# Cross-attention of a two-layer Perceiver on one core: decay scans in another place, high halves of the context tiles by ACT, and a re-ordered start

## The reference, cut to what matters

```python
x = x + L0_xattn(layernorm(x), ctx_2048, Wq, Wk, Wv)      # x (2,128,256), ctx (2,2048,256)
# 32 heads of 8: q, k = per-head rmsnorm(x Wq.T), rmsnorm(ctx Wk.T); v = ctx Wv.T
# out = softmax(q k.T * 8**-0.5) v
x = x + L0_attn(layernorm(x), ...)
x = x + L0_ffn(layernorm(x), ...)
x = x + L1_xattn(layernorm(x), ctx_2048, decay, W_in, b_in, W_out, b_out, gamma, beta)
#   K = sigmoid(decay); s_t = K * s_{t-1} + (W_in ctx_t + b_in); mean over t of W_out s_t + b_out
x = x + L1_attn(layernorm(x), ...)
x = x + L1_ffn(layernorm(x), ...)
```

## Time and profile before

| what | us |
|---|---|
| median of three runs | 450.17 |
| the profiled execution's own time | 449.79 |
| its span, first to last instruction | 448.0 |
| PE busy | 399.9 (89%) |
| DVE busy | 310.7 (69%) |
| ACT busy | 250.4 (56%) |
| POOL busy | 221.3 (49%) |

### The profile page before, as it was taken

The page is one execution under the profiler, slowest core; times in us unless marked ns, Lnnn a source line. Parts: engine busy times, 40 slices in busy tenths (PEclk is TensorE's granted clock), DMA queues, the critical chain, the costliest instruction groups (busy, mean ns, idle before and its releaser), DMA issues.

```text
span 448.0 us, 12553 instructions
## 1 busy us (share of the span) xinstructions
PE 399.9 (89%) x5149; PEld 333.5 (74%) x5149; DVE 310.7 (69%) x697; ACT 250.4 (56%) x494; POOL 221.3 (49%) x269
## 2 busy tenths in 40 slices
PE   6769999999999999879979977789789888999997
PEld 4546666677667777678979955668679877889996
DVE  5677878887888786557798876574998967322221
ACT  2447878778887888775545514521923044544541
POOL 2267656666666773334544620510489742544440
PEclk9979999999999999999999989999899999999999
DMA  4076651543311101620000080250000052000000
GB/s 149 0 262 229 206 172 45 164 127 91 105 32 44 30 15 47 247 113 1 0 1 2 1 321 3 79 244 1 0 2 1 1 227 102 1 0 2 0 2 23
DMA packets 10537, 34.67 MB, mean 77 GB/s; under 512 B 2160, under 2 KB 7280, under 8 KB 8688
## 3 DMA queue, kind: packets, MB, share of 16 engines
q1 hardware_dynamic: 10336, 33.34, 21.4%
q10 hardware_dynamic: 144, 0.52, 0.5%
HBM read 33.60 MB, written 0.26 MB: 76 GB/s over the span
## 4 chain that ended last, share of the span: by engine, by line
PE 52%; DVE 27%; POOL 10%; ACT 5%; issue 4%; DMA 1%; SPq 0%; DVEq 0%; POOLq 0%; ACTq 0%
PE ps L1075 7%; PE ps L1576 7%; PE ps L1532 6%; PE ps L1061 6%; PE ps L1546 3%; PE ps L395 3%; DVE sb_big L1315 2%; PE ps L1563 2%; POOL sb_arena L984 2%; PE ps L456 2%; PE ps L381 2%; DVE sb_arena L1325 2%; PE ps L746 2%; POOL sb_mid L998 2%; DVE sb_big L1313 2%
## 5 line engine op out<-in xcount | busy, mean ns | idle before, releaser
L1499 ACT ACTIVATE sb_arena<-ps 128x1024 f32<-128x1024 f32 x128 | 123.4, 1020 | 26.4 <-PE ps L1563 26.3
L1576 PE MATMUL ps<-sb_arena 128*25 128x128 f32 (+1 forms) x2048 | 69.4, 276 | 0.3 <-ACT sb_arena L1499 0.3
L1576 PEld LDWEIGHTS ps<-sb_arena 128*25 128x25 f32 (+1 forms) x2048 | 50.7, 98 | 7.7 <-ACT sb_arena L1499 0.8
L1532 PE MATMUL ps<-sb_halves 128*128 128x512 f32 x192 | 55.4, 425 | 0.9 <-DVE sb_arena L1325 0.9
L1105 POOL TENSOR_TENSOR sb_halves<-sb_big,sb_halves 128x704 fp32r<-128x704 f32 x20 | 33.7, 1687 | 38.8 <-ACT sb_halves L1099 38.8
L485 POOL TENSOR_TENSOR sb_halves<-sb_big,sb_halves 128x256 fp32r<-128x256 f32 x32 | 23.7, 760 | 44.9 <-ACT sb_halves L469 44.9
L1171 DVE SCALAR_TENSOR_TENSOR sb_arena<-ps,sb_w_q,sb_arena 128x176 f32<-128x176 f32 x40 | 15.9, 401 | 42.7 <-ACT sb_arena L1123 42.5
L1532 PEld LDWEIGHTS ps<-sb_halves 128*128 128x128 f32 x192 | 35.3, 197 | 13.5 <-issue 5.9
L1398 POOL TENSOR_TENSOR sb_big<-sb_arena 128x256 f32<-128x256 f32 x31 | 19.0, 613 | 52.3 <-DVE sb_arena L1286 52.3
L1075 PE MATMUL ps<-sb_halves 128*128 128x352 f32 x240 | 42.9, 332 | 2.0 <-POOL sb_halves L1105 2.0
L1075 PEld LDWEIGHTS ps<-sb_halves 128*128 128x128 f32 x240 | 39.1, 189 | 3.3 <-DVE sb_arena L1171 1.7
(11 more groups left out here) (223 smaller groups left out, 871.0 us busy)
## 6 DMA issues: line engine op xcount, KB each, us to landing
sb_big<-in_w_gu SPq DMA_DIRECT2D x2, 3520.0 KB, 11.8
sb_arena<-in_ctx SPq DMA_DIRECT2D x32, 128.0 KB, 2.3
sb_mid<-in_w_down SPq DMA_DIRECT2D x1, 3584.0 KB, 12.7
sb_mid<-in_w_ffn SPq DMA_DIRECT2D x3, 768.0 KB, 5.3
sb_big<-in_w_q SPq DMA_DIRECT2D x2, 1024.0 KB, 6.5
sb_big<-in_w_k SPq DMA_DIRECT2D x2, 1024.0 KB, 7.1
sb_big<-in_w_v SPq DMA_DIRECT2D x2, 1024.0 KB, 6.0
sb_mid<-in_w_o SPq DMA_DIRECT2D x2, 1024.0 KB, 6.0
```

The lines of the kernel that those rows point to most:

```text
L1499: nc.scalar.activation(probs[:, n % P_SLOTS].rearrange("p a g n -> p a (g n)"), ps[:, bank:bank + 2], ACT.Exp, scale=XD ** -0.5).then_inc( ...
L1532: i = T.matmul(ps[:, 7], ctx_half[:, t % 2, c, kt], wkv_half[:, d, kt], start=(n + kt == 0), stop=(n == 2 and kt == KT - 1))
L1576: i = T.matmul(ps[32 * gg:32 * gg + m, 6, j * P:(j + 1) * P], v_sb[:, t % V_SLOTS, 4 * gg + j, head], probs[:, n % P_SLOTS, a, gg], start= ...
```

## The change

Seven edits, all in the cross-attention stage:

1. DVE: the decay rate and the first scan move from behind the packing of tile 1 to the start; the scan of tile t + 2 moves from the head of step t to behind `take_v(t + 2)`, ahead of `mean_squares(t + 2)`.
2. The high half of context tiles 4 to 31 is made by ACT (`split_high`), behind the third exponential of step t for tile t + 4, and no longer by POOL. POOL still makes the low half and waits for the high one.
3. The values of tile 0 are taken by ACT instead of DVE.
4. The queries of the second batch are taken by ACT a little later, behind `key_rstd(0)`.
5. ACT loads its function table ahead of the DMA of `w_xkv`, and issues the DMA of `w_xq` behind it, which SP issued before.
6. PE makes `project(1)` ahead of the transposes of the queries.
7. PE gets 20 more unread matmuls at the start, in groups of 6, 4, 6 and 4.

```diff
-            sp.dma_start(w_xq, io["w_xq"]).then_inc(sem("wq_loaded"), 16)
...
+            decay_rate()
             mean_squares_q(0)
+            decay_weights(0)
             take_k(0)
             norm_q(0)
             mean_squares(0)
             pack_q(0)
-            take_v(0)
             pack_keys(0)
             take_k(1)
             take_keys(0)
             take_v(1)
             mean_squares(1)
+            decay_weights(1)
             pack_keys(1)
-            decay_rate()
-            decay_weights(0)
-            decay_weights(1)
             for t in range(NB):
-                if t + 2 < MB:
-                    decay_weights(t + 2)
                 if t + 2 < NB:
                     take_k(t + 2)
                     take_v(t + 2)
+                    if t + 2 < MB:
+                        decay_weights(t + 2)
                     mean_squares(t + 2)
...
-                if t >= 2:
-                    pool.wait_ge(sem("kv_projected"), t - 1)
-                G.tensor_copy(ctx_half[:, t % 2, 0], ctxT[:, t % CTX_SLOTS]).then_inc(sem("ctx_high"), 1)
+                if t < 4:
+                    if t >= 2:
+                        pool.wait_ge(sem("kv_projected"), t - 1)
+                    G.tensor_copy(ctx_half[:, t % 2, 0], ctxT[:, t % CTX_SLOTS]).then_inc(sem("ctx_high"), 1)
                 pool.wait_ge(sem("ctx_high"), t + 1)
...
+            nc.scalar.preload_act_table_set("natural_log_exp_and_others")
             act.dma_start(w_xkv, io["w_xkv"]).then_inc(sem("wkv_loaded"), 16)
-            nc.scalar.preload_act_table_set("natural_log_exp_and_others")
+            act.dma_start(w_xq, io["w_xq"]).then_inc(sem("wq_loaded"), 16)
...
-            take_queries(1)
+            act.wait_ge(sem("v_cleared"), 1)
+            for r in range(2):
+                i = nc.scalar.copy(v_sb[:, 0, :, 25 * r:25 * r + 8],
+                                   ps[:, 7, 256 + 128 * r:384 + 128 * r].rearrange("p (h d) -> p h d", d=XD))
+            i.then_inc(sem("kv_taken"), 1)
...
+            def split_high(t):
+
+                act.wait_ge(sem(f"ctx_loaded{t % CTX_SLOTS}"), 16 * (t // CTX_SLOTS + 1))
+                act.wait_ge(sem("kv_projected"), t - 1)
+                nc.scalar.copy(ctx_half[:, t % 2, 0], ctxT[:, t % CTX_SLOTS]).then_inc(sem("ctx_high"), 1)
...
             key_rstd(0)
+            take_queries(1)
...
                     exps(SUBS * t + c)
+                    if c == 2 and t + 4 < NB:
+                        split_high(t + 4)
...
             ln_transpose(pe, LN_OF["xattn"], 0)
+            keep_warm(6, 6)
...
+            keep_warm(4, 6)
             open_acc()
+            project(1)
+            keep_warm(6, 0)
             pe.wait_ge(sem("id16_loaded"), 16)
             pe.wait_ge(sem("q_packed"), 1)
             turn_queries(0, 4)
-            project(1)
+            keep_warm(4, 0)
             turn_keys(0)
```

More of the change, by code:

```diff
@@ L1234, in _ @@
             V.memset(xnT[:, :, :, 0:3], 0.0)
-            step(dve, V.memset(v_sb, 0.0))
+            V.memset(v_sb, 0.0).then_inc(sem("v_cleared"), 1)
+            dve.wait_ge(sem("v_cleared"), 1)
             V.memset(v_sb[:, :, :, 8:9], 1.0)
```

## The result

| | kernel before | changed kernel |
|---|---|---|
| median, us | 450.3 (449.66 to 450.70, 4 runs) | 460.46 (458.94 to 461.12, 4 runs) |
| profiled execution, its span | 449.79, 448.0 | 460.0, 458.1 |
| mean granted clock of PE | 0.985 | 0.974 |

At the very start its row is not to be relied on: in the kernel before it says 1.00 from 9 to 12 us, where PE's products take the durations that they have at half clock (experiment 7). So 0.985 is an upper bound.

The account below looks back on a forecast made before the run. No engine alone bounds the cross-attention. With e(t) the start of tile t's third exponential, e(27) = 25.3 + 141.1 + 2.95 - 0.82 = 168.5 against 166.8, less 0.5: +1.2 on 449.79, forecast 451.3 us, range 445.0 to 454.7.

Parts of the forecast that it names:

- the clock: Rival: POOL's stall in packing the second queries reaches PE and brings half clock, 452.8 to 454.3 us; chance 0.16.
- the end: From third exponential of tile 27 to first of tile 29: 6.93 us instead of 7.40, giving back 0.47.
- the steps without a scan: Cross-attention main loop: 14 steps of 5.11 us each, the bare loop of 5.05 plus 0.06.
- the stall: POOL's packing of the second batch's queries stands in the loop once and costs 2.95 us.
- the start: Up to the third exponential of tile 0: it comes at 25.3 us instead of 27.38.
- The loop through POOL, DVE and ACT: Cross-attention main loop: POOL's wait for ACT's cast closes a round of 5.05 us, longer than PE's 4.81.
- the step with a scan: Cross-attention main loop: 13 steps of 5.35 us each, with 0.24 for the scan.
- the two collisions: In the loop's step: packing's last copy on POOL's low half 0.06 us, scan ahead of POOL's next square 0.24.
- a bare loop: Rival: main loop at its bare 5.05 us a step without collisions, 446.7 us; chance 0.21.
- a PE-bound one: Rival: the loop doesn't bind and PE sets 4.81 us a step everywhere, near 438.5 us; chance 0.06.
- the poor start: Rival: unread matmuls delay the first projection and x lands no earlier, 453 us; chance 0.08.
- the whole scans: Rival: each scan in the main loop costs POOL its whole 0.48 us, 3.1 more, 454.4 us; chance 0.05.

Follow-up runs that it names:

- experiment 7: The changed kernel without its 20 added unread matmuls; 460.53 us, ratio 1.021 to the kernel before.
- experiment 3: The changed kernel with ACT's cast behind the first exponential instead of the third; 444.18 us, ratio 0.988 to the kernel before.
- experiment 4: The changed kernel with ACT's cast behind the fourth exponential instead of the third; 480.54 us, ratio 1.068 to the kernel before.
- experiment 8: The changed kernel with matmuls of zeros added into the open accumulator in three idle gaps of PE; 459.22 us, ratio 1.020 to the kernel before.
- experiment 5: The changed kernel with POOL's square of tile 5 ahead of packing the second batch's queries; 458.0 us, ratio 1.016 to the kernel before.
- experiment 2: The kernel before with edit 2 alone, high halves of tiles 4 to 31 by ACT behind the third exponential; 463.0 us, ratio 1.027.
- experiment 1: The changed kernel with all high halves made by POOL again (edit 2 undone); 444.94 us, ratio 0.989 to the kernel before.
- experiment 9: The changed kernel with the cast behind the first exponential, plus zeros in PE's gaps, tile 5's square earlier and DVE's four weight sums moved; 444.8 us, ratio 0.986.
- experiment 10: The changed kernel with high halves on POOL, plus zeros in PE's gaps, tile 5's square earlier and DVE's four weight sums moved; 444.26 us, ratio 0.986.
- experiment 6: The kernel before with the first edit alone, decay rate and scans in their new places; 446.48 us, ratio 0.991.

## Why the prediction was right and wrong

The forecast was 9 us short. In its own terms: the clock, put at nothing in the sum, +3.4 in the steps and +1.35 at the end; the steps without a scan +2.8; the odd step at tile 6 +1.6; the rest of the end +1.6; the stall -0.2; the start -1.7.

**Right: the mechanism.** The loop through POOL, DVE and ACT closes as described and binds both batches (experiments 3 and 4). The forecast 5.05 for its bare length from single rows of before; the second batch shows 0.65 + 0.45 + 0.40 + 0.90 + 0.54 + 0.85 + 0.80 + 0.69 = 5.28. Two terms were small by 0.24 together: low half to product 0.85 for 0.69, because DVE's last copy of the packing falls on it (priced 0.06, cost 0.16), and the cast to POOL 0.54 for 0.46. Over the 14 steps without a scan that and one longer step at tile 16 (5.69) make 2.8 of the missed 7.6.

**Right by two errors: the step with a scan.** 5.35 was forecast and 5.35 came. But the scan cost POOL nothing: the product beside it takes 0.73, the sum 0.73. The scan itself was stretched, from 0.48 to 0.59, and DVE's sum of squares comes 0.71 behind the square instead of 0.65, which no run explains. The 0.24 and 0.06 booked for the two collisions were really the copy's 0.16, the 0.08 between cast and POOL, and this 0.06.

The Trainium skill, SBUF — State Buffer (Who interferes with whom), says that an operation of DVE with two SBUF inputs contends with one of GpSimd that reads SBUF, that the lock is exclusive, and that the order of issue decides who blocks. The forecast left out the order and put the whole 0.48 on POOL. Here POOL's product had started at 81.82 and the scan came at 82.24; by the rule the scan should have waited until 82.55, an estimate of 0.31 from these rows. The trace agrees on who pays and not on the amount: the scan lost 0.11, and POOL kept its 0.73. The cost of a collision has to be given to one of the two, and I gave it to the wrong one.

**Wrong, and the largest: the half clock was priced as a rival and stood at nothing in the sum.** This is the step of the forecast that failed first: 13 x 5.35 takes every step of the first batch at full clock. The forecast named the rival ("Three microseconds at half clock or more cost 1.5 to 3") and gave it 0.16. It came twice in the first batch. Experiment 8, with the gaps filled, shows both: 0.83, 0.92, 0.82 and 0.78 in four steps, 3.35 in all. The text argued that PE's idle 3.44 had come before half clock in the kernel before, and that the stall of 2.95 would go through to PE; both held. The first of the two is not even new: the kernel before has its half clock in the same steps (6.31 and 6.25), hidden in its average of 5.16. So 1.75 of the 3.35 was in the kernel before as well, and only the 1.6 behind the stall is new. The statement "no half clock before 34 us" was wrong too: PE's idle times of 1.49 and 1.02 just ahead of 23.9, with one group of transposes (0.61) between them, came before it here.

**Wrong: a step left out.** At tile 6 the queries of the second batch are transposed in the same bank as the keys; that step took 6.57 before, and 6.98 now, 1.6 above its neighbours. The average of before hid it in 5.16; a sum built from single steps has to list the odd ones.

**Nearly right: the stall.** 2.95 forecast, the step of 8.10 is 2.75 above 5.35. So the first 13 steps are 3.35 (clock) + 1.63 (tile 6) - 0.2 (stall) = 4.8 over the forecast.

**Wrong: the start, by 1.7 to the good, and in part by the luck of the profile.** The forecast priced the unread matmuls as a delay of 0.35 and took PE's first projections at the durations of before. In this profile they ran at full clock (1.13 for 2.08), and e(0) came at 23.62; in the profiles of experiments 4 and 5, with the same start and those durations, it came at 25.31 and 25.16, where the forecast had 25.3. The table load did not hold back the DMA behind it: the DMA was issued at 0.76 while the load ran from 0.73 for 1.28, and DVE's first work on x came 0.13 earlier, not 0.5.

**Wrong: the end.** -0.5 was forecast, +2.5 came. In three parts. The last cast, behind e(27), still holds one more round, so the next two steps take 5.28 + 4.53 where the forecast let PE's pace begin at once: 7.59 to the first exponential of tile 29 for 6.93, 0.66 missed. Then PE stood still for no wait that the profile shows ("issue"):

```profile
182.01 1.94 ACT L1510 ACTIVATE sb_arena<-ps 128x1024 f32<-128x1024 f32 x2 [0.39 <-PE ps L1577]
...
191.00 0.42 PE L1590 MATMUL ps<-sb_arena 128*25 128x128 f32 x8 [0.78 <-issue]
...
195.57 0.77 PE L1599 MATMUL ps<-sb_id,sb_theta 128*128 128x128 f32 x4 [0.55 <-DVE sb_theta L1332]
```

Before, the same way from exponential to transposes took 186.93 - 174.22 = 12.71, here 13.56, 0.85 more. And the attention stage got one more stretch of half clock; the way from 240 to 250 us has a mean clock of 0.83 with 7.69 us of PE work in 10:

```profile
240.00:250.00 10.00, 7.69 (x49) 7.31 (x49) 7.71 (x18) 2.66 (x10) 3.47 (x4) 0.83 0.00 0
```

That is 1.35 us, by how far equal rows of the two kernels lie apart ahead of it (8.65) and behind it (10.00). The time behind e(27) varies between 281.2 and 286.4 over kernels that are nearly equal there, so this term could not have been forecast closely, but a spread of some 2 us for it belonged in the range.

**The chances.** Slower was given 0.52 against 0.32 for faster. The faster rivals, a bare loop and a PE-bound one, were closed by the terms that the forecast itself had added up. The range ended at 454.7 as if only one of the clock, the poor start and the whole scans could come.

## What to carry to other kernels

When work moves to another engine to relieve the first, write down the round that closes over the two and compare it with the pace of the bound engine, not with the busy times: a cast of 0.40 cost 15 us behind the third exponential and nothing behind the first. Look for the latest point of the other engine's program that is not behind work which itself waits for you. Where a new wait makes PE idle for 1 to 3 us, look for half clock behind it and give it a term. Here the two steps behind such waits lost 1.75 and 1.6 us in the changed kernel, 0.5 at the start of experiment 5 and behind the stall of experiment 2, and nothing in experiment 4, whose loop left PE time to spare. And don't read one profile's start as the kernel's: with the same start e(0) came anywhere from 23.6 to 25.3.

## What was not expected of the hardware

- Matmuls of zeros in the idle gaps kept the granted clock at 1.00 from 12 to 58 us (experiment 8), and took away 3.3 us of step time that the changed kernel's profile lost. The median fell by 1.2, which is not resolved.
- A wait of PE is not by itself followed by half clock. In experiment 4 PE waited 1.19 to 2.72 us in every step from 59 to 118 us, and the granted clock stayed at 1.00 up to 128 us; its next half clock came behind a wait of 1.64 at 128.2. The later part of it:

```profile
90.00:128.00 38.00, 29.50 (x676) 21.36 (x668) 22.07 (x59) 27.55 (x45) 16.93 (x25) 1.00 0.34 103
```

- One and the same program differs in its half clock from run to run. Runs of the kernel before took 447.81 us at a mean clock of 0.992 and 454.49 at 0.966; runs of experiment 8 456.38 at 0.992 and 460.89 at 0.974. By the profiled clocks the changed kernel had 2 x 0.026 x 458.1 = 23.8 us at half clock and the kernel before 13.4, the latter without the half clock of its first projections, which its clock row misses.
- PE stopped for 0.5 to 1.2 us near the end of the cross-attention, put down to no wait, in the changed kernel (0.78) and in experiments 1, 3, 4, 5, 9 and 10. It did not in the kernel before and in 2, 6, 7 and 8. The first lot have 20 or 34 matmuls more in PE's program ahead of that place than the kernel before, the others none, and 8 has 44. What causes it stays open; no run was made for it.
- A scan of 128x128 that meets POOL's work took 0.58 to 0.95 as a rule instead of 0.48, and up to 1.03 once in some kernels, while POOL's product lost 0 to 0.12. A plain fp16 copy of 128x512 that begins with POOL's subtraction cost POOL 0.16.
